# Self-attention by query halves, with a lead of 14 units, and all operand transfers and the second group's copies on GpSimd

## What is computed

```python
x_norm = modulate(_ln(x), shift_a, scale_a)
qkv = x_norm @ W_qkv + b_qkv                       # NH = 16 heads of hd = 16 features
attn_w = softmax(einsum('bhqd,bhkd->bhqk', q, k) * scale)
attn_out = einsum('bhqk,bhkd->bqhd', attn_w, v)    # 1024 queries x 1024 keys per head
x = x + gate_a[:, None] * (attn_out.reshape(B, N, H) @ W_proj + b_proj)
```

## Time and profile before

| | us |
|---|---|
| median of three runs (lowest to highest) | 1603.7 (1603.05 to 1605.82) |
| the profiled execution, its own time | 1601.8 |
| its span | 1600.0 |
| self-attention of sequence 0: first query unit to first key unit | 248.29 to 283.26 |
| its units with both roles | 283.26 to 422.59 |
| its units with key scores alone, to the last copy of the result | 422.59 to 453.29 |

### The profile page before, as it was taken

The page is one execution under the profiler, slowest core; times in us unless marked ns, Lnnn a source line. Parts: engine busy times, 40 slices in busy tenths (PEclk is TensorE's granted clock), DMA queues, the critical chain, the costliest instruction groups (busy, mean ns, idle before and its releaser), DMA issues.

```text
span 1600.0 us, 26614 instructions
## 1 busy us (share of the span) xinstructions
PE 1490.6 (93%) x10593; PEld 937.2 (59%) x10593; DVE 1050.8 (66%) x2960; ACT 769.6 (48%) x1232; POOL 377.6 (24%) x419
## 2 busy tenths in 40 slices
PE   5899999999999999987999999999999999998898
PEld 3457765444355857656765767544445475765676
DVE  2574456999537446899457535599972745579963
ACT  1335421788844533325543543168885363333454
POOL 4420006342125110114133000634210701001330
PEclk9999999999999999999999999999999999999999
DMA  9500037121020000000130001812102000000000
GB/s 339 164 0 1 0 112 106 21 42 22 2 79 1 1 0 3 2 1 1 46 125 1 1 1 61 157 22 36 27 2 79 1 1 1 2 2 1 1 1 27
DMA packets 37663, 59.81 MB, mean 37 GB/s; under 512 B 7347, under 2 KB 27091, under 8 KB 36643
## 3 DMA queue, kind: packets, MB, share of 16 engines
q1 hardware_dynamic: 25239, 34.71, 6.6%
q0 software_dynamic: 9520, 16.04, 6.2%
q10 hardware_dynamic: 2780, 7.36, 1.3%
HBM read 42.22 MB, written 2.10 MB: 28 GB/s over the span
## 4 chain that ended last, share of the span: by engine, by line
PE 66%; DVE 21%; issue 6%; ACT 3%; DMA 1%; POOL 1%; ACTq 0%; DVEq 0%; POOLq 0%
PE ps L999 10%; PE ps L1011 9%; PE ps L463 5%; PE ps L1321 4%; PE ps L984 3%; PE ps L591 3%; PE ps L1112 3%; DVE taken L2384 3%; DVE rs L2062 3%; PE ps L1346 2%; PE ps L1103 2%; DVE taken L2396 2%; DVE mxw L2054 2%; PE ps L1173 2%; PE ps L599 2%
## 5 line engine op out<-in xcount | busy, mean ns | idle before, releaser
L2251 DVE TENSOR_REDUCE mm<-ps 128x1 f32<-128x1024 f32 x256 | 310.5, 1223 | 35.1 <-PE ps L984 31.7
L1640 ACT ACTIVATE pt<-ps 128x512 f32<-128x512 f32 x512 | 276.8, 600 | 61.0 <-PE ps L999 43.6
L2502 POOL TENSOR_TENSOR rstd<-ve,minus_half 128x4 f32<-128x4 f32 x32 | 34.9, 1091 | 695.3 <-DVE ve L1926 695.3
L999 PE MATMUL ps<-qx,kx 64*128 64x512 f32 x512 | 188.5, 445 | 1.0 <-ACT pt L1640 1.0
L984 PE MATMUL ps<-kx,qx 48*128 48x512 f32 x512 | 186.7, 444 | 0.2
L1011 PE MATMUL ps<-pt,v 128*32 128x256 f32 x2048 | 158.7, 390 | 0.0
L999 PEld LDWEIGHTS ps<-qx,kx 64*128 64x128 f32 x512 | 79.0, 184 | 95.9 <-ACT pt L1640 85.9
L591 PE MATMUL ps<-filler 128*128 128x512 f32 x382 | 119.8, 440 | 0.0
L2139 DVE TENSOR_TENSOR rlo<-ring,rhi 128x512 fp32r<-128x512 f32 x48 | 33.2, 691 | 91.9 <-ACT ring L1590 91.9
L1011 PEld LDWEIGHTS ps<-pt,v 128*32 128x32 f32 x2048 | 42.9, 108 | 85.5 <-ACT pt L1640 61.3
L984 PEld LDWEIGHTS ps<-kx,qx 48*128 48x128 f32 x512 | 75.4, 185 | 24.4 <-issue 19.3
(11 more groups left out here) (374 smaller groups left out, 3319.7 us busy)
## 6 DMA issues: line engine op xcount, KB each, us to landing
wm<-in_L_xcond_W_mlp_dram SPq DMA_DIRECT2D x4, 1024.0 KB, 8.6
qx<-q_hi POOLq DMA_DIRECT2D x64, 64.0 KB, 2.5
kx<-k_hi POOLq DMA_DIRECT2D x64, 64.0 KB, 2.5
w3a<-in_L_xcond_w_m_dram SPq DMA_DIRECT2D x2, 2048.0 KB, 7.6
w<-in_L_xcond_e_w_dram SPq DMA_DIRECT2D x6, 512.0 KB, 7.9
w<-in_L_xcond_e_w_dram SPq DMA_DIRECT2D x2, 1536.0 KB, 12.8
s_ada<-in_L_xcond_w_ada_dram ACTq DMA_DIRECT2D x1, 2304.0 KB, 23.3
qx<-q_lo POOLq DMA_DIRECT2D x32, 64.0 KB, 2.4
```

Source lines behind the costliest of these rows:

```text
L999: pe.matmul(ps[:, bank, :], kx[r, p % 4, kc * P:(kc + 1) * P], qx[r, p % 4, half * 512:(half + 1) * 512], start=True, stop=True).then_inc( ...
L1640: act.activation(pt[:, u % 8, half * 512:(half + 1) * 512], ps[:, bank, :], ACT.Exp, scale=QK_SCALE).then_inc(st_read, 1)
L2251: return dve.tensor_reduce(mm[:, p % 2, e, t:t + 1], place(), X, ALU.max).then_inc(ring_read, 1)
```

## The change

1. `LEAD` falls from 22 to 14.
2. A key unit covers one half of the queries (512) and two key tiles, where it covered one key tile and all queries. `u < 8` is the first half of the queries, `u >= 8` the second. So maxima are written, turned, copied and moved by halves: twice as often, four tiles at a time, with two DMAs where there were four. `weigh_values` reads its 256 columns as two runs of 128.
3. The first eight query units (pair 0) take one tile of queries against half of the keys, for both heads at once, so that units 0 to 3 need only token block 0. Its operands are spread by halves: first block 0 (16x512), then k and q of block 1. POOL starts on them before the second `ln`.
4. POOL waits for the fill to land (`fill_ld`) before it issues any row of maxima; before, PE alone waited for it.
5. `spread(2)` and `spread(3)` come after the first rows of maxima; later spreads are split into a q part and a k part around the rows.
6. POOL makes the high copies of the second group too (two casts of 128x1024), in the turn of pair 1.
7. The values of block 1 and the second group's projections move into query units 0 to 9, and the filler of the start goes: of 9, 4 and 7 fillers ahead of the loop none is left, and of 3 per turn in 18 turns two per turn in two turns.

```diff
-N_MROW = 4 * 16
+N_MROW = 2 * 16
-LEAD = 22
+LEAD = 14
...
-                keep_busy(6, 9)
+                full_step(0)
+                full_step(1)
                 ln(2, 1)
-                keep_busy(6, 4)
+                full_step(2)
...
                 def query_scores(p, u):
                     bank = take()
+                    if p == 0 and u < T:
+                        for e in range(2):
+                            r, t, half = slice(64 * e, 64 * e + 3 * HD), u % TB, u // TB
+                            ins = pe.matmul(ps[:, bank + e, :], qx[r, 0, t * P:(t + 1) * P], kx[r, 0, half * 512:(half + 1) * 512],
...
+                def key_scores(p, u, i):
+                    half, e, kc = u // T, u % 2, 2 * (u % T // 2) + i
...
+                        weights = pt[:, (2 * w + e) % 8, i * BLK:(i + 1) * BLK].rearrange("p (j a c) -> p j a c", a=2, c=P)
+                        for part in range(2):
+                            o = 32 * (2 * e + part)
+                            ins = pe.matmul(ps[o:o + 32, 7, half * 2 * P:(half + 1) * 2 * P], v2[:, kc, ...],
+                                            weights[:, :, part, :], ...)
...
-                        if u == 0:
-                            pe.wait_ge(mrow_ld[p % 2], b * N_MROW * NP // 2 + N_MROW * (p // 2 + 1))
+                        if u % T == 0:
+                            pe.wait_ge(mrow_ld[u // T], (b * NP + p + 1) * N_MROW)
                         key_scores(p, u, 0)
...
-                    if m >= 4 and n < 4:
-                        keep_busy(4 if m < 2 * T else 7, 3 if n < 0 else 1)
+                    if m >= 12 and n < 4:
+                        keep_busy(5 if n < 0 else 7, 2 if n < 0 else 1)
...
-                    if at_m == 1 and 1 <= q <= NP:
-                        turn_maxima(q - 1)
+                    if at_m == 9 and q < NP:
+                        turn_maxima(q, 0)
+                    elif at_m == 1 and 1 <= q <= NP:
+                        turn_maxima(q - 1, 1)
...
-                for i in range(4):
-                    act.wait_ge(spread_ld[i], b * 2 * N_SPR + N_SPR)
-                for qk in range(2):
-                    act.activation(dense[2 * qk][:, :], full[qk], ACT.Copy).then_inc(hi_ready, 1)
...
-                        if at_m == 2 * T - 1:
-                            maxima(q)
+                        if m == TB - 1:
+                            add_v2(1)
+                        if at_m % T == T - 1:
+                            maxima(q, at_m // T)
...
+                def maximum_rows(p, half):
+                    pool.wait_ge(st_read, b * N_KEY + key_entries(p, half))
                     for e in range(2):
+                        r = 64 * e + 3 * HD
+                        pool.dma_start(qx[r:r + 2, p % 4, half * BLK:(half + 1) * BLK]..., mxT[T * e:T * (e + 1), half, :]).then_inc(mrow_ld[half], 16)
...
+                part(0, 0, 0, low, first_ld)
+                ln(2, (1,))
+                pool.wait_ge(hi_ready, b * 6 + 2)
+                part(1, 0, 0, low, first_ld)
...
+                pool.wait_ge(first_ld, b * N_FIRST + N_SPR)
+                pool.wait_ge(hi_ready, b * 6 + 3)
+                part(1, 0, 0, high, first_ld)
...
-                spread(3)
+                pool.wait_ge(fill_ld, b * 64 + 64)
                 for p in range(NP):
-                    maximum_rows(p)
+                    maximum_rows(p, 0)
                     if p == 0:
+                        spread(2)
+                    elif p == 1:
...
                         for qk in range(2):
+                            pool.tensor_copy(dense[2 * qk][:, :], full[qk]).then_inc(hi_ready, 1)
                             pool.tensor_tensor(dense[2 * qk + 1][:, :], full[qk], dense[2 * qk][:, :].bitcast(F32), ALU.subtract)...
+                    elif p + 3 < NP:
+                        spread(p + 3, (0,))
+                    maximum_rows(p, 1)
```

More of the change, by code:

```diff
@@ L87, with turns_before, key_entries @@
 R_G_A, R_G_SA, R_G_CA, R_BP0, R_B_A, R_BCP, R_B_SA, R_B_CA = range(N_ROW)
-def key_entries(p):
-    return 2 * max(0, 2 * T * (p + 1) + 2 - LEAD) + p + 1
+def turns_before(m):
+    return sum(2 * T * p + T * half + 9 < m for p in range(NP) for half in range(2))
+def key_entries(p, half):
+    return 2 * max(0, 2 * T * p + T * half + 10 - LEAD) + 2 * p + half + 1
 def bursts_of(n):
@@ L160, in build @@
         mm = keep("mm", [P, 2, 2, T])
-        mhl = keep("mhl", [P, 2, 2, 2, T], F32R)
-        mxT = keep("mxT", [4 * T, 2, P], F32R)
+        mhl = keep("mhl", [P, 2, 2, 2, 2, T // 2], F32R)
+        mmq = keep("mmq", [P, 2, 2, T // 2])
+        mxT = keep("mxT", [2 * T, 2, P], F32R)
         filler = keep("filler", [P, BLK], F32R)
@@ L1000, in key_scores, with weigh_values @@
                               start=True, stop=True).then_inc(st_ready, 1)
-                def weigh_values(w, part):
-                    p, kc = w // T, w % T
+                def weigh_values(w, i):
+                    p, half, kc = w // T, w % T // TB, 2 * (w % TB) + i
                     pe.wait_ge(st_read, b * N_KEY + entry_of[2 * w + 1])
-                    if kc == 0 and part == 0 and p >= 1:
+                    if kc == 0 and half == 0 and p >= 1:
                         pe.wait_ge(acc_read, b * NP + p)
                     for e in range(2):
[L1009 to L1013, removed]
+                        weights = pt[:, (2 * w + e) % 8, i * BLK:(i + 1) * BLK].rearrange("p (j a c) -> p j a c", a=2, c=P)
+                        for part in range(2):
+                            o = 32 * (2 * e + part)
+                            ins = pe.matmul(ps[o:o + 32, 7, half * 2 * P:(half + 1) * 2 * P], v2[:, kc, VS * (2 * p + e):VS * (2 * p + e) + 32],
+                                            weights[:, :, part, :], start=kc == 0 and half == 0, stop=kc == T - 1 and half == 1)
+                    if i == 1:
                         ins.then_inc(pv2_done, 1)
@@ L1053, in _ @@
[L1053 to L1056 removed]
+                        if m == 0:
+                            pe.wait_ge(first_ld, b * N_FIRST + N_SPR)
+                        elif m == TB:
+                            pe.wait_ge(first_ld, b * N_FIRST + N_FIRST)
+                        elif m == T:
+                            pe.wait_ge(spread_ld[0], b * (first + 2 * N_SPR) + first)
+                        elif at_m == 0:
+                            pe.wait_ge(spread_ld[q % 3], loads[q])
@@ L2521, in _, with part @@
                 ln(1)
-                ln(2)
-                def spread(p):
+                ln(2, (0,))
+                def part(qk, part, p, cols, done):
+                    wide = (qx, kx)[qk]
+                    for e in range(2):
+                        r = 32 * (p % 4) + HD * e
+                        for i in range(3):
+                            if ((0, 1, 0), (0, 0, 1))[qk][i] == part:
+                                pool.dma_start(wide[64 * e + HD * i:64 * e + HD * (i + 1), p % 4, cols], dense[2 * qk + part][r:r + HD, cols]).then_inc(done, 16)
@@ L2560, in _ @@
                 pool.memset(v2[:, :, 0:H * VS].rearrange("p t (h d) -> p t h d", d=VS)[:, :, :, HD:VS], 1.0).then_inc(v2_clear, 1)
-                for p in range(3):
-                    spread(p)
+                pool.wait_ge(lo_ready, b * 4 + 1)
+                part(0, 1, 0, low, first_ld)
+                pool.wait_ge(lo_ready, b * 4 + 2)
+                part(1, 1, 0, low, first_ld)
+                pool.wait_ge(first_ld, b * N_FIRST + N_SPR)
+                pool.wait_ge(hi_ready, b * 6 + 3)
+                pool.sem_inc(passed, 1)
+                part(1, 0, 0, high, first_ld)
+                pool.wait_ge(ring_read, b * N_RING + 1)
+                part(1, 1, 0, high, first_ld)
+                pool.wait_ge(hi_ready, b * 6 + 4)
+                part(0, 0, 0, high, spread_ld[0])
+                pool.wait_ge(ring_read, b * N_RING + 2)
+                part(0, 1, 0, high, spread_ld[0])
+                spread(1)
                 pool.wait_ge(v_done, b * NB + NB)
```

223 lines of the change are left out of this document (126 added, 97 removed).

## The result

The changed kernel takes 1592.62 us (four executions, 1590.26 to 1596.12) where the kernel before takes 1604.76 on the same chip: a ratio of **0.9924, 95% interval 0.9899 to 0.9949**. That is 12.1 us less; 23.2 were forecast. The time lies just inside the upper end of the range, and outside the forecast's own 1567 to 1589. The profiled execution of the changed kernel is the slowest of its four, 1596.12 with a span of 1594.3.

The account below looks back on a forecast made before the run. The first key unit's start was taken to bound the stage: 16.7 gained, less 2.4 for the clock and 2.7 for maxima, 11.6 us per sequence, 23.2 in both, from 1603.7 to 1580.5 us. Range 1563 to 1593, its own 1567 to 1589.

Parts of the forecast that it names:

- What bounds the stage: Self-attention stage: what matters is when the first key unit starts; the stage ends 170 us after it.
- The first operands and the lead: Stage start: query unit 0 some 7.5 us earlier, DVE sets the pace, PE has nothing left from about 259.4.
- The fill: Before the first rows of maxima: POOL waits for a landing 9.9 us after issue; first key unit at 266.6, 16.7 gained.
- The first rival: Fill lands like spreads, 2.6 us after issue; no clock lost, 19.6 us gained per sequence, 1564.5 us; chance 0.15.
- The clock: After PE's 7.2 us idle before the first key unit: half speed costs 2.4 us per sequence, between 0 and 3.4.
- the second rival: Clock falls already in the lead: first key unit about 274, 5 us gained per sequence, 1594 us; chance 0.10.
- the clock falls already in the lead: The second rival: without filler PE runs the lead's 14 units at half speed; 1594 us, chance 0.10.
- The extra maxima: Units of both kinds: eight more writings of maxima on DVE cost 2.7 us per sequence, between 0 and 4.3.
- Priced at nothing: Charged zero: ACT's two lost copies, POOL's two casts, the wait in later q spreads, value matmuls reading two runs.
- the third rival: Value matmuls, 1024 per sequence, pay for two runs: at 20 ns each, slower at 1621 us; chance 0.05.
- The fourth rival: First operands land 17 us late behind weights SP loads, POOL shifts everything: no earlier start, 1609 us; chance 0.04.

Follow-up runs that it names:

- the three fillers: Changed kernel with three fillers instead of one in each of key units 0 to 3; 1601.64 us in a single execution.
- A + B: Changed kernel plus eight fillers before the first operands, thirty before the first key unit, four for two in the lead's last two turns; 1581.84 us, ratio 0.9859.

## Why the prediction was half right

**What bounds the stage: right.** The time goes with the start of the first key unit, and the stage behind it keeps its length at full clock: 172.0 against 170.0.

**The first operands and the lead: right, a little early.** Unit 0 was put 7.5 us earlier and came 6.1 earlier, with the whole stage of the profiled execution 0.87 later. PE's lead ends at 260.8 (forecast 259.4). What was mis-sized is the landing of the first operands: 2.6 us were taken from the earlier trace rows, a stretch in which the core's DMA moved 53 GB/s (239 to 242); after the change they are issued while it moves 292 to 371 GB/s (228 to 239) and land after 3.8 to 6.3. That the traffic is the reason was not tested. So POOL goes on at 242.71, where 240.5 was forecast:

```profile
242.71 1.92 POOL L2582 DMA_DIRECT2D kx<-k_hi  x4 [4.31 <-DMA kx<-k_lo]
```

**The fill: right.** 9.9 was taken, the last landing is 9.6 after its issue, and the rows leave POOL after an idle time of 9.69. The first rival is out. By the Trainium skill (DMA: Bandwidth & Descriptors, Anatomy of one DMA) 256 KB were an estimate of 2.6 us; the trace of the changed kernel has 5.0 to 9.6, where that of the kernel before has 4.6 to 9.9. Cut by pairs into 64 KB (an estimate of 2.2 by that fit) they land like this, in the kernel that also moves the gates:

```profile
DMA to landing us min/median/max: 2.3/2.6/5.0
```

The start of the first key unit, 268.23, is 1.6 later than forecast, half of it the later stage and the rest the late first operands, which put the fill off. The first rival's step "PE idles 1.6 us, so no clock is lost" would not have held either: with the fill by pairs a wait of 1.71 us was followed by half speed until 283.

**The clock: this step failed.** From one early stretch I took it that the clock is back 4.9 us after work returns, and charged 2.4 us per sequence, at most 3.4. It was back after 17.8 and 19.3 us. With the clock held and nothing else of the order changed (A + B) the stage is 172.00 and 172.03; the changed kernel's 179.02 and 182.09 are **7.0 and 10.1 us** longer, 17.1 in all against the 4.8 charged. In sequence 1 this also holds 1.7 at most for a short fall at 1197 to 1201 (half speed for 3.4 us in sum) and 0.76 of a late row of maxima. The difference of 12.3 is the main part of the gain that is missing. Between the two profiled executions (spans of 1600.0 and 1594.3) 17.5 of the 23.2 are missing: 12.3 here; 2.4 by the first key units, which gain 15.9 and 15.1 from the start of their stage (ACT's first `q_hi` at 228.19 and 996.20 before, 229.06 and 991.27 after) where 16.7 was forecast; 4.3 in the stages before, between and behind, which the change does not touch; less 1.4 by the maxima. Between the medians 11.1 are missing. That 1592.62 lies in the range at all, by 0.4 us, is luck: the range reaches beyond 1589 only for the sake of the second rival, and the clock's term was more than three times too small.

So one stretch of another stage was taken for a rule. What follows the two pauses differs: a matmul over 128 rows, here score matmuls over 48 and 64 rows with one filler to each unit. In the changed kernel the clock rose 5.8 and 7.3 us after the first value matmuls, which are over 128 rows (280.23 and 1043.24); in every fall that lasted into the key units, in all runs, it rose 2.1 to 8.0 us after them. Against this as the reason speak the three fillers, which brought it back no sooner, and the lead of the kernel with filler in the wait: there the projections of the values and of the second group, over 128 rows, stood between the scores from 244.4 on, and the clock still rose only at 262.6. Why it came back after 5 us in one place and after 18 in the other stays open.

**The rival "the clock falls already in the lead"** was set aside with "the idle pieces are far shorter than the 6.05 us that are on record". This argument was wrong: falls came behind a pause of 1.53 us in one kernel, and in another where the longest pause was 0.24. In the profiled execution of the changed kernel the clock fell only behind the lead; with the lead of 18, and with the fill by pairs and the gates moved, it fell in the lead.

**The extra maxima: somewhat dear.** 2.7 was taken; the stage at full clock is 2.0 longer. That these 2.0 are the maxima's was not tested.

**Priced at nothing: right.** The value matmuls take 391 ns each at full clock (group of the changed kernel between 310 and 400 us, where the kernel before has 390), so the third rival is out:

```profile
L1031 PE MATMUL ps<-pt,v 128*32 128x256 f32 x544 | 42.7, 391 | 0.0
```

POOL's two casts (1.06 and 1.03) and the subtractions lie between the rows of 292.44 and 302.48. The fourth rival's cause is there in small: the first operands do land late while the weights are loaded, and PE stands 0.50 us ahead of unit 0 here and up to 2.52 in other kernels of the experiments; the 17 us that it needs are not there.

## What to carry to other kernels

Filler whose result nobody reads can hold the clock up in stretches of small score matmuls: whoever removes it with a shorter lead has to cost the clock of the next 20 us as well as the pause, and should measure the new order with filler put back before judging it. Remove the wait ahead of the critical unit too (here by cutting a 256 KB fill to the part that is needed first): against the changed kernel this alone gave 6 us, filler alone 11, both with the gates' copy moved 23. Take a transfer's landing time from a stretch with the same DMA traffic: 2.6 us became up to 6.3 here. Where the executions of one kernel spread by 2% along with their mean granted clock, the clock falls in some of them, and the median of a few says little about the order.

## What the hardware showed

**The clock falls without a long pause.** It fell to half where PE's longest pause in the 12 us ahead was 0.24 us, and in a lead where it was 0.33. The Trainium skill (TensorE: Matmul & The Clock Gate, HAM oscillation) explains falls by idle gaps of PE; the traces here have falls in or behind gaps (7.40, 5.69, 1.53 us) and falls with none to speak of.

**It returns late.** The Trainium skill (TensorE: Matmul & The Clock Gate, What's actually happening) has it that activity releases the throttle. Here PE worked without a pause at 1.2 GHz for 17.8 and 19.3 us from the first key unit on before it rose, 17.5 and 22.2 with three fillers per unit; with the fill by pairs it rose 18.5 and 14.6 after that unit. There the Trainium skill also calls the moment dependent on the run; the traces agree in so far as the two sequences of one execution differ by 1.5 to 4.7 us.

**A cast that takes six times as long.** While POOL's subtraction for `k_lo` ran, DVE's cast of 8 columns took 1.02 us, and 0.17 to 0.23 elsewhere. DVE and POOL timelines of the changed kernel:

```profile
299.55 1.02 DVE L2307 CAST mhl<-mm 128x8 fp32r<-128x8 f32 x1
...
385.25 0.17 DVE L2307 CAST mhl<-mm 128x8 fp32r<-128x8 f32 x1
```
```profile
298.14 2.41 POOL L2651 TENSOR_TENSOR k_lo<-hT,k_hi 128x1024 fp32r<-128x1024 f32 x1
```

It ends with the subtraction, at 300.57 and 300.55. The Trainium skill (SBUF — State Buffer, Who interferes with whom) says that such a cast and a GpSimd instruction can share a pair of ports, and that the one that comes second waits for the whole of the other; the trace agrees, in sequence 1 too. The cast is 0.85 us longer, once per sequence; what that costs the kernel no run here shows.
